# A four-layer graph network on one core: attention passes over 202 quads of edge tiles instead of 204

## The reference

```
h = x
for _ in range(STEPS):                                   # STEPS = 2
    edge_feat = concatenate([h[src], h[dst]], axis=-1)   # 100000 x 256
    messages = _mlp2(edge_feat, msg_W1, msg_b1, msg_W2, msg_b2)
    att = sigmoid(_mlp2(edge_feat, att_W1, att_b1, att_W2, att_b2))
    aggregated = segment_sum(messages * att, dst, num_segments=num_nodes)
    new_h = _mlp2(concatenate([h, aggregated], axis=-1), upd_W1, upd_b1, upd_W2, upd_b2)
    h = new_h + h + global_repr
```

## Time and profile before

| | us |
|---|---|
| median of 3 runs | 6523.08 (6523.01 to 6523.32) |
| the profiled execution | 6518.71 |
| its span, first to last instruction | 6517.0 |
| PE busy | 5097.5 (78%) |
| DVE busy | 3210.5 (49%) |
| POOL busy | 2411.9 (37%) |
| ACT busy | 1691.7 (26%) |
| mean granted TensorE clock | 0.868 of full speed |

### The profile page before, as it was taken

How to read it: one execution, slowest core, us unless ns; L and a number is a source line. 1 busy time by engine, 2 the same in 40 slices (tenths; PEclk the granted TensorE clock), 3 DMA queues, 4 the chain that set the end, 5 groups by cost and what they waited for, 6 DMA issues and landing times. The chain is left out here.

```text
span 6517.0 us, 95366 instructions
## 1 busy us (share of the span) xinstructions
PE 5097.5 (78%) x29088; PEld 3386.5 (52%) x29088; DVE 3210.5 (49%) x8514; ACT 1691.7 (26%) x4273; POOL 2411.9 (37%) x2524
## 2 busy tenths in 40 slices
PE   3555777999998878887998999999999987444443
PEld 1334555888875667776444444444444444333333
DVE  5887996888876777776653212111121123122221
ACT  3006995555543333333001011010010012000000
POOL 0780003666745777774000000000000002777776
PEclk7658998999998999998999999999999998555555
DMA  3457997555544444443854554544535524111112
GB/s 112 158 164 262 326 327 246 161 161 161 161 116 125 130 130 131 131 130 75 311 192 177 192 177 146 193 155 167 195 133 188 196 71 177 53 53 53 53 53 57
DMA packets 460315, 1009.70 MB, mean 155 GB/s; under 512 B 66081, under 2 KB 309718, under 8 KB 449494
## 3 DMA queue, kind: packets, MB, share of 16 engines
q1 hardware_dynamic: 348454, 711.13, 32.2%
q0 software_dynamic: 111536, 293.76, 15.9%
HBM read 768.42 MB, written 236.21 MB: 154 GB/s over the span
## 5 line engine op out<-in xcount | busy, mean ns | idle before, releaser
L1870 POOL DMA_INDIRECT ring<-rows,stage x1428 | 1369.4, 959 | 1116.3 <-ACT stage L1929 604.1
L1723 POOL DMA_INDIRECT ring<-rows,stage x808 | 764.3, 946 | 2711.5 <-ACT stage L1707 2465.6
L1366 PE MATMUL ps<-strip,trans_part 128*128 128x512 f16 (+1 forms) x8232 | 1606.0, 356 | 23.1 <-DVE trans_part L1283 23.1
L1366 PEld LDWEIGHTS ps<-strip,trans_part 128*128 128x128 bf16 x8232 | 755.5, 98 | 927.7 <-issue 76.9
L1955 PE MATMUL ps<-here,spread 128*128 x3264 | 955.0, 417 | 217.0 <-DVE ring L1904 180.8
L1775 PE MATMUL ps<-ring,mark 128*128 128x128 f32 x1616 | 414.4, 438 | 584.9 <-DMA ring<-rows,stage 583.6
L1904 DVE TENSOR_TENSOR ring<-ring,ps 128x512 f32<-128x512 f32 x816 | 561.0, 688 | 403.7 <-PE ps L1955 238.0
L1975 PE MATMUL ps<-ring,mark 128*128 128x128 f32 x3264 | 734.9, 313 | 3.4 <-issue 0.5
L1955 PEld LDWEIGHTS ps<-here,spread 128*128 128x128 f32 x3264 | 575.3, 196 | 310.8 <-issue 256.2
L1775 PEld LDWEIGHTS ps<-ring,mark 128*128 128x128 f32 x1616 | 357.1, 326 | 642.3 <-issue 642.3
L1275 DVE TENSOR_TENSOR trans<-ps,be 128x512 f32<-128x512 f32 x96 | 66.3, 691 | 1185.3 <-PE ps L1356 1185.3
(11 more groups left out here) (342 smaller groups left out, 5399.5 us busy)
## 6 DMA issues: line engine op xcount, KB each, us to landing
strip<-adj SPq DMA_DIRECT2D x392, 800.0 KB, 4.2
adj<-piece SPq DMA_DIRECT2D x120, 640.0 KB, 4.0
locs<-loc_rows SPq DMA_DIRECT2D x420, 128.0 KB, 3.1
ahead<-ahead_piece SPq DMA_DIRECT2D x125, 320.0 KB, 4.1
back<-back_piece SPq DMA_DIRECT2D x125, 320.0 KB, 4.5
sheet<-ahead SPq DMA_DIRECT2D x25, 1600.0 KB
sheet<-back SPq DMA_DIRECT2D x25, 1600.0 KB
ring<-rows,stage POOLq DMA_INDIRECT x2236, 2.5
```

The costliest lines, as they stand in the source:

```text
L1366: last = eng.matmul(k.ps[:, b, 0:cols], part[:, (step * NW + w) % TABLES, m, t * D:(t + 1) * D], strip[:, at % RING, c0:c0 + cols], start= ...
L1723: eng.indirect_dma_start(ring[:, t, :], None, rows, bass.IndirectOffsetOnAxis(stage[:, t:t + 1], 0)).then_inc(s_full[q], 16)
L1870: eng.indirect_dma_start(ring[:, t, :], None, rows, bass.IndirectOffsetOnAxis(stage[:, t:t + 1], 0)).then_inc(s_full[q], 16)
```

## The change

The attention passes run `NQUADS` = 202 quads. That is 33 turns of six and four quads behind them, written out on every engine. POOL's and ACT's loops have 33 turns instead of 34. DVE's loop keeps 33 turns, and what is written out behind it is four quads instead of six. SP's loop has 32 turns, and four quads follow in which the ring is refilled too; nothing is fetched for quads that do not exist. PE's code is that of before without the last two quads. The waits for landed DMAs at the end count by slot. Buffers, tiles, waits within a quad and all other phases are as before.

```diff
-    in_body, bodies = QUAD * NQ, NT // (QUAD * NQ)
+    in_body = QUAD * NQ
+    bodies, rest = divmod(NQUADS, NQ)
@@ SP
-            def turn(i, more):
-                for q in range(NQ):
+            def turn(i, quads):
+                for q in range(quads):
                     eng.wait_ge(s_spread, i * NQ + q + 1)
                     fetch(i * in_body + in_body + q * QUAD, q)
-                    if more and early is not None:
+                    if early is not None:
                         eng.wait_ge(s_done, i * NQ + (NQ + q + 1))
                         refill(i * NQ + (NQ + q), q)
...
             with eng.Fori(0, bodies - 1) as i:
-                turn(i, True)
-            turn(bodies - 1, False)
+                turn(i, NQ)
+            turn(bodies - 1, rest)
             for q in range(NQ):
-                eng.wait_ge(s_locs[q], 16 * (bodies + 1))
+                eng.wait_ge(s_locs[q], 16 * (bodies + (q < rest)))
@@ POOL (the body of quad is that of the loop before)
             with eng.Fori(0, bodies) as i:
                 for q in range(NQ):
+                    quad(i, q)
+            for q in range(rest):
+                quad(bodies, q)
             for q in range(NQ):
-                eng.wait_ge(s_full[q], bodies * landed)
+                eng.wait_ge(s_full[q], (bodies + (q < rest)) * landed)
@@ DVE
-                        if q + 1 < NQ:
+                        if q + 1 < quads:
                             spread_quad(i, q + 1, g + 1)
-                        elif not last:
+                        elif more:
                             spread_quad(i + 1, 0, g + 1)
...
-            with eng.Fori(0, bodies - 1) as i:
-                body(i, False)
-            body(bodies - 1, True)
+            with eng.Fori(0, bodies) as i:
+                body(i, NQ, True)
+            body(bodies, rest, False)
@@ PE
-                    more = q + LAG < NQ or not last
+                more = g + LAG < NQUADS
...
-                        if j == 2 and g + LAG + 1 < NT // QUAD:
+                    if j == 2 and g + LAG + 1 < NQUADS:
...
-            for i in range(bodies):
-                body(i, i == bodies - 1)
+            for g in range(NQUADS):
+                quad(g, g % NQ)
```

More of the change, by code:

```diff
@@ L1861, in _, with quad @@
         def _(eng):
+            def quad(i, q):
+                eng.wait_ge(s_staged, i * NQ + q + 1)
+                eng.wait_ge(s_done, i * NQ + q + 1)
+                eng.sem_inc(s_go, 1)
+                for j in gathered:
+                    t = q * QUAD + j
+                    eng.indirect_dma_start(ring[:, t, :], None, rows,
+                                           bass.IndirectOffsetOnAxis(stage[:, t:t + 1], 0)).then_inc(s_full[q], 16)
             with eng.Fori(0, bodies) as i:
                 for q in range(NQ):
[L1864 to L1871, removed]
+                    quad(i, q)
+            for q in range(rest):
+                quad(bodies, q)
             for q in range(NQ):
-                eng.wait_ge(s_full[q], bodies * landed)
+                eng.wait_ge(s_full[q], (bodies + (q < rest)) * landed)
         @block.vector
@@ L1881, in spread_quad, with body @@
                 eng.tensor_scalar(spread[:, q, :], locs[:, q, :], k.lane[:, 0:1], None, ALU.is_equal).then_inc(s_spread, 1)
-            def body(i, last):
-                for q in range(NQ):
+            def body(i, quads, more):
+                for q in range(quads):
                     g = i * NQ + q
@@ L1929, in _, with quad @@
                 eng.activation(stage[:, q * QUAD:(q + 1) * QUAD], index(q * QUAD, QUAD), ACT.Copy).then_inc(s_staged, 1)
+            def quad(i, q):
+                g = i * NQ + q
+                eng.wait_ge(s_full[q], i * landed + landed)
+                eng.activation(stage[:, q * QUAD:(q + 1) * QUAD], index(i * in_body + in_body + q * QUAD, QUAD),
+                               ACT.Copy).then_inc(s_staged, 1)
+                eng.wait_ge(s_dot, g * QUAD + QUAD)
+                eng.activation(att[:, q * QUAD:(q + 1) * QUAD, 0], dot[:, q * QUAD:(q + 1) * QUAD], ACT.Sigmoid,
+                               bias=b_att[:, 0:1]).then_inc(s_att, 1)
+                eng.wait_ge(s_att, g + 1)
+                for j in range(QUAD):
+                    t = q * QUAD + j
+                    eng.activation(ring[:, t, 0:D], ring[:, t, 0:D], ACT.Relu, scale=att[:, t, 0:1]).then_inc(s_msg, 1)
             with eng.Fori(0, bodies) as i:
                 for q in range(NQ):
[L1932 to L1943, removed]
+                    quad(i, q)
+            for q in range(rest):
+                quad(bodies, q)
         @block.tensor
@@ L1957, in expand @@
                 last.then_inc(s_exp, 1)
-            def body(i, last):
-                for q in range(NQ):
-                    g = i * NQ + q
-                    more = q + LAG < NQ or not last
[L1963 to L1970, removed]
-                        if j == 2 and g + LAG + 1 < NT // QUAD:
[L1973 to L1980, removed]
@@ new lines, in quad @@
+            def quad(g, q):
+                more = g + LAG < NQUADS
+                now, scalar = found[g]
+                if more:
+                    eng.wait_ge(s_spread, g + (LAG + 1))
+                for j in range(QUAD):
+                    if more and j % 2 == 0:
+                        expand(g + LAG, (q + LAG) % NQ, j // 2, found[g + LAG][0])
+                    if j == 0:
+                        eng.wait_ge(s_mark, g + 1)
+                    if j == 2 and g + LAG + 1 < NQUADS:
+                        found[g + LAG + 1] = tiles.load(g + LAG + 1)
+                    eng.wait_ge(s_msg, g * QUAD + (j + 1))
+                    eng.matmul(k.psf[:, bass.ds(now[j], D)], mark[:, q, j, :], ring[:, q * QUAD + j, 0:D],
+                               start=False, stop=False, skip_group_check=True)
+                    done = eng.matmul(k.psf[:, bass.ds(scalar[j], 2)], mark[:, q, j, :],
+                                      att[:, q * QUAD + j, :], start=False, stop=False,
+                                      skip_group_check=True)
+                done.then_inc(s_done, 1)
```

## The result

The changed kernel took 6502.82 us (median of 6 runs, 6493.54 to 6509.73) against 6525.28 for the kernel before in the same set: 22.5 us less, a ratio of 0.9964 (95% interval 0.9951 to 0.9977). The forecast was 22.5 less than 6523.08, 6500.6 us. The sum fits the medians. The traces show that its second term does not fit as well as that, and in part why.

A forecast was written before the change was run, and what follows sets the result against it. PE was taken to bound the first attention pass, POOL's issue the second until late landings at its end. Savings of 8.4 + 14.1 = 22.5 us from 6523.1 gave 6500.6 us, range 6494.6 to 6508.6.

The forecast's parts named there:

- The bound of each pass: First attention pass bound by PE at 4.10 us a quad, second by POOL's gather issue at 5.06 us a quad.
- First pass, 8.4 us: First attention pass: two quads less move PE's work up by 8.40 us, bounds 8.2 to 9.0.
- table loads: ACT in the first pass: 33 loads per line instead of 34, worth 0; rival 2.6 us more saved, chance 0.04.
- Second pass, 14.1 us: Second attention pass: quad 201's add stays at 3017.31 and replaces the last at 3031.43, saving 14.12 us, bounds 10.2 to 15.5.
- what took 6.3 us from the add to the end follows it instead: End of second pass: the 6.3 us after the old last add now follow quad 201's add unchanged.
- 5 us for the clock: Allowance either way for two stretches of PE at half clock, as work moves in time.
- the low end: Second pass lower bound: a last landing always 7.91 us behind its issue, so POOL's pace saves only 10.2 us.
- loops' ends: POOL and ACT leave their loops after 33 turns with four quads to do; cost taken as 0.
- fetches: SP's locs strips, 202 a pass instead of 210: the 16 removed are unread, cost nothing, give at most 1.38 us.
- The issue rate: Rival, second pass: whichever quad is last lands late, so 18.6 us saved in all, 6504.5 us; chance 0.15.
- The clock's case: Rival: shifted later stages get four or more extra half-clock stretches, 10 us, giving 6510.6 us; chance 0.05.
- A stall behind the loops: Rival: POOL or ACT waits for instructions after its loop, four times 14.5 us, giving 6558.6 us; chance 0.02.

The follow-up runs named there:

- e10_178_quads: The changed kernel with 178 quads in both passes instead of 202: 6895.31 us against 7202.65 for the kernel before in that set, ratio 0.9571.
- e2_form204: The changed kernel's loops but all 204 quads in both passes: 6523.80 us against 6523.65 for the kernel before, ratio 0.9998.
- e4_second202: The changed kernel's loops with 202 quads in the second pass only, 204 in the first: 6513.21 us, ratio 0.9982 to the kernel before.
- e1_again: The changed kernel run again without edit: 6501.98 us against 6523.65 for the kernel before, ratio 0.9964.
- e3_first202: The changed kernel's loops with 202 quads in the first pass only, 204 in the second: 6515.95 us against 6523.65 for the kernel before.
- e7_no_reload: The changed kernel with one sigmoid of a constant ahead of ACT's loop, so one table load in the first pass: 6499.99 us against 6525.92 for the kernel before.
- e6_pad_rows_202: The changed kernel with partition p's padding reading row p instead of row 0: 6505.27 us against 6525.92 for the kernel before.
- e12_pads_table_again: The changed kernel without table reloads and with padding rows spread where padding is first set, run a second time: 6492.30 us against 6522.11 for the kernel before.
- e5_pad_rows_204: The changed kernel's loops with 204 quads, partition p's padding reading row p instead of row 0: 6519.45 us against 6525.92 for the kernel before.

## Why the prediction was right, and which term was not

**The bound of each pass: right.** PE's pace in the first, POOL's issue in the second, and the price of a removed quad goes by them. The clearest evidence is the pair with spread padding, in which no landing is late at the end: two quads are worth 8.4 us in the first pass (863.6 and 855.2) and 10.0 in the second, against 8.2 and 10.1 by the steady pace. The 11.8 us of e10_178_quads agrees with its set's pace of 11.95, but in that set PE does not bound the first pass, so it shows nothing of the bounds.

**First pass, 8.4 us: right in kind, a little small.** Three traces with 204 quads (before, e2_form204, e4_second202) take 863.8, 863.5 and 863.6 us, three with 202 (after, e1_again, e3_first202) 854.2, 855.1 and 855.0. That is 8.9 us, inside the 8.2 to 9.0 given. The half microsecond beyond the two rows read is less than the 202-quad traces differ among themselves (0.9 us). The table loads give at most a part of it: two of the traces with 204 quads have 33 a line already.

**Second pass, 14.1 us: the mechanism right, the term too large.** With padding on row 0 the pass takes 1046.9, 1049.0 and 1051.3 us with 204 quads (mean 1049.1), and 1042.4, 1036.1, 1040.9 and 1040.9 with 202 (after, e1_again, e4_second202, e7_no_reload; mean 1040.1): 9.0 less. Its parts: eight gathers at 1.27 us, 10.1, as worked out. The last landing comes 7.91, 6.58 and 6.75 us behind its issue with 204 quads and 3.63, 3.71, 5.07 and 3.82 with 202: 3.0 less, where the prediction had 3.9 from the single trace of before. Against these stand the tail, in which the clock was low in one of three traces with 204 quads and in three of four with 202 (2.2 us in the mean), and a pace that lay 2 ns a gather higher (1.9 us). That the higher pace belongs to the change is not shown, since the paces of the two kinds of trace overlap. For the low clock, one trace in three against three in four is little to go by. The step that failed is "what took 6.3 us from the add to the end follows it instead". It took 10.8 where PE had idled for 2.9 us. The prediction did allow 5 us for the clock, but as a matter of chance with either sign, and it priced the tail by its fast form. The very row it leaned on, the landing that is late by itself, is what lets PE idle at the end. The 9.0 us measured are nearer to the 10.2 that the prediction took as the low end than to its 14.1.

**The sum.** By the traces the two passes together are worth 8.9 + 9.0 = 18 us, by the medians 22.5 and 21.7; the intervals of the latter reach from 14 to 32 us, so both can stand. The two kernels with one pass each changed give 7.7 + 10.4 = 18.1 by their medians. That 22.5 was met to the tenth is luck, and which of 18 and 22 is the worth of the change stays open. The profiled execution of before, 6518.71 us, is faster than all of the 33 runs of its kernel in the two sets of the changed one, which took 6520.58 to 6531.41; the changed one's first profiled run is the slowest of its six. So that pair of traces shows 9 us, which is too little for the change.

**What was costed at nothing was nothing:** loops' ends (e2_form204), table loads (e2_form204, and e7_no_reload: 1 to 2 us for 65 of them), fetches (12 of the 16 are gone in e2_form204). The Trainium skill (ScalarE: Activation LUTs, "What ACT_TABLE_LOAD costs") puts 2.66 us on a switch of tables. The measurement decides against taking that as a price here: ACT had the time to spare, and the copy behind a load starts as it ends.

**The rivals.** The issue rate as a mechanism fell: in every trace with 202 quads and padding on row 0 the last landing was 3.6 to 5.1 us behind its issue and not 7.9, and spreading the padding's rows brought the last landing to 1.8 us behind its issue (e6_pad_rows_202, e12_pads_table_again), and with that it is true that two quads are worth POOL's pace. As a number the rival did well: its 18.6 us is what the traces give. The clock's case did happen in part, 4.8 us in the first trace. A stall behind the loops was not seen.

## What to carry to other kernels

Price the removal of a loop's last turns by the pace of the engine that bounds the pass, then read the tail by itself: who waits there, and at which clock the waiting engine resumes. Padding indices that all point at one row make gathers slow exactly at the end of a pass, where nothing covers them; spread them. Where executions differ by 5 to 10 us, take each stage's length from several traces before a term of 4 us is believed, since one trace has one pace and one pattern of the clock.

## What the runs showed of the hardware

- Gathers of one row by all partitions: the gathers' queue took 87.1% of the engines' time for 0.63 MB in 8 us against 35.1% for 2.21 MB in 22. When each partition read a row of its own, it took 34.7% for 0.81 MB in the 8 us of the same quads (e5_pad_rows_204), and a last landing 3.6 to 7.9 us behind its issue fell to 1.8 (e6_pad_rows_202, e12_pads_table_again).
- PE's clock in the tail of the second pass: 1.2 GHz for most of it in four traces in which DVE's last wait for a landing was 2.42 to 4.19 us, 2.4 GHz in five in which it was 0.15 to 2.36 us, and 2.4 GHz in one with a wait of 2.88 us and 2.54 us of matmuls of zeros in the gap. Elsewhere the clock fell behind 2.30 us of idle time of PE and did not behind 2.48 us, so the length alone does not tell.
- The same program took 6522 to 6526 us in four sets and 7203 in one. In a trace of another kernel from the slow set PE waits for nothing that the profile shows ahead of single matmuls (443.7 us in the last pass over the edges), and the same kernel has no such waits there in another set. What holds PE up there is open.
